# FFN weights loaded first and quantised as they land; V copied from PSUM by ScalarE, its bias folded into the output projection's

## What is computed

```
def fp4_linear(x, w):
    xq = fp4_quant_dequant(x)
    wq = fp4_quant_dequant(w)
    return einsum('bsk,nk->bsn', xq, wq)
...
v = (x @ Wv + bv).reshape(Bb, Ss, H, HD)
...
attn = softmax(scores, axis=-1)
out = einsum('bhts,bshd->bthd', attn, v).reshape(Bb, Ss, Dd)
return out @ Wo + bo
```

## Time and profile before

| | |
|---|---|
| median of 3 runs | 4952.22 us (4935.51, 4952.22, 4952.87) |
| the profiled execution | 4937.85 us, of which the span from first to last instruction is 4936.0 us |
| mean granted TensorE clock | 0.907 |
| TensorE busy | 3986.5 us (81%) |
| VectorE busy | 4018.3 us (81%) |
| ScalarE busy | 2381.1 us (48%) |
| GpSimd busy | 1575.5 us (32%) |
| the chain that ended last | PE 38%, DVE 38%, ACT 11%, issue 4%, DMA 4%, SPq 3% |

### The profile page before, as it was taken

How to read it: one execution, slowest core, us unless ns; L and a number is a source line. 1 busy time by engine, 2 the same in 40 slices (tenths; PEclk the granted TensorE clock), 3 DMA queues, 4 the chain that set the end, 5 groups by cost and what they waited for, 6 DMA issues and landing times.

```text
span 4936.0 us, 53882 instructions
## 1 busy us (share of the span) xinstructions
PE 3986.5 (81%) x18173; PEld 2036.9 (41%) x18173; DVE 4018.3 (81%) x5964; ACT 2381.1 (48%) x4341; POOL 1575.5 (32%) x1036
## 2 busy tenths in 40 slices
PE   3456768898988888888988888888989888877767
PEld 1222324353535444443535444443535344434343
DVE  5487879898898989899898989898988989785512
ACT  1334344546545465545555464645465454543332
POOL 0043333333433333333433333333334333333000
PEclk9667879999999999999999999999999999898877
DMA  1387666767767776767777677677677677774100
GB/s 56 82 181 186 147 169 157 181 162 169 179 149 184 160 184 163 175 163 171 177 159 177 157 186 171 165 169 179 170 163 176 152 185 161 182 175 92 41 22 29
DMA packets 241433, 753.39 MB, mean 153 GB/s; under 512 B 37650, under 2 KB 132659, under 8 KB 171524
## 3 DMA queue, kind: packets, MB, share of 16 engines
q1 hardware_dynamic: 241156, 749.95, 63.5%
HBM read 647.30 MB, written 101.71 MB: 152 GB/s over the span
## 4 chain that ended last, share of the span: by engine, by line
PE 38%; DVE 38%; ACT 11%; issue 4%; DMA 4%; SPq 3%; POOL 1%; DVEq 0%; ACTq 0%; POOLq 0%
DVE state L1559 9%; PE m L1087 7%; DVE mt L1647 6%; PE m L1059 6%; DVE u L1554 5%; DVE front L1496 2%; PE m L1099 2%; DVE front L1381 2%; SPq L551 2%; PE pd L1284 2%; DMA dt_scratch<-front 2%; PE y L1162 2%; DVE front L1383 2%; DVE front L1469 1%; DVE front L1472 1%
## 5 line engine op out<-in xcount | busy, mean ns | idle before, releaser
L708 POOL TENSOR_TENSOR state<-state,bc 128x1024 f32<-128x1024 f32 x512 | 1216.2, 2376 | 1886.2 <-DVE u L1554 1886.2
L1559 DVE TENSOR_TENSOR_SCAN state<-decay,u 128x1024 f32<-128x1024 f32 x512 | 1169.2, 2284 | 24.0 <-ACT decay L878 11.1
L878 ACT ACTIVATE decay<-decay,a_neg 128x511 f32<-128x511 f32 x1024 | 670.1, 711 | 169.5 <-DMA decay<-dt_scratch 168.8
L1059 PE MATMUL m<-w_gu,hats_m 128*128 128x480 f32 (+1 forms) x1536 | 686.4, 579 | 28.9 <-DVE front L1472 23.1
L1554 DVE TENSOR_TENSOR u<-state,bc 128x1024 f32<-128x1024 f32 x512 | 645.5, 1261 | 44.4 <-DMA state<-dtx_scratch 36.5
L1087 PE MATMUL m<-w_dn,front 128*128 128x256 f32 (+1 forms) x1536 | 424.7, 423 | 17.9 <-ACT front L814 16.4
L692 POOL TENSOR_TENSOR front<-front,hsc_m 128x704 f32<-128x704 f32 x128 | 192.0, 1500 | 728.0 <-DVE front L1383 728.0
L1059 PEld LDWEIGHTS m<-w_gu,hats_m 128*128 128x128 f32 x1536 | 281.7, 195 | 300.4 <-issue 208.3
L1151 PE MATMUL y<-state,sel 128*32 128x512 f32 x2048 | 290.9, 651 | 122.5 <-POOL state L708 121.7
L795 ACT ACTIVATE front<-m 128x240 f32<-128x240 f32 (+1 forms) x384 | 137.2, 362 | 500.4 <-PE m L1059 478.0
L1087 PEld LDWEIGHTS m<-w_dn,front 128*128 128x128 f32 (+1 forms) x1536 | 301.5, 208 | 141.0 <-issue 65.7
(11 more groups left out here) (260 smaller groups left out, 7112.8 us busy)
## 6 DMA issues: line engine op xcount, KB each, us to landing
decay<-dt_scratch SPq DMA_DIRECT2D x256, 1024.0 KB, 7.2
state<-dtx_scratch SPq DMA_DIRECT2D x256, 1024.0 KB, 11.3
qk_scratch<-shared SPq DMA_DIRECT2D x64, 384.0 KB, 3.5
shared<-qk_scratch SPq DMA_DIRECT2D x384, 64.0 KB
kh<-qk_scratch SPq DMA_DIRECT2D x384, 64.0 KB
xs_scratch<-front SPq DMA_DIRECT2D x16, 1024.0 KB, 6.0
dt_scratch<-front SPq DMA_DIRECT2D x256, 64.0 KB, 2.0
dtx_scratch<-hats_m SPq DMA_DIRECT2D x256, 64.0 KB, 1.7
```

Of the source, the lines that this page charges most:

```text
L708: eng.tensor_tensor(st, st, bc[:, 1:2, :].to_broadcast([P, WIDE, L]), ALU.mult).then_inc(scan_pool.sem, scan_pool.step(f"c{r}{h}"))
L878: ins = eng.activation(d, d, ACT.Exp, scale=a_neg[:, g:g + 1])
L1059: mm = eng.matmul(f.bank(f"gu{t}{p}")[:, 0:2 * width], f.norm.hat_t[:, k, t * P:(t + 1) * P], w_gu[:, k, 2 * lo:2 * (lo + width)], start=( ...
L1559: eng.tensor_tensor_scan(st, decay[:, n % ND, h * WIDE * L:(h + 1) * WIDE * L], u[:, :], 0.0, ALU.mult, ALU.add).then_inc(scan_dve.sem, sc ...
```

## The change

1. The loads of the three FFN weights are issued ahead of the first sequence, and each weight has a semaphore of its own (`raw_loaded`). VectorE waits for that alone before it quantises a weight; its wait for `loaded` and the small copy `raw_by_state` come after the three. TensorE and ScalarE still wait for all of `loaded` at their start.
2. `bv` is loaded as a column per feature, and `bo` as one row. In the setup TensorE computes `bv @ Wo + bo` (three matmuls, 1x256), ScalarE copies it into `bo`, and only then comes the rest of ScalarE's setup.
3. V is copied from PSUM by ScalarE instead of being added to `bv` by VectorE. The plan tables are unchanged, so that the four copies have no entry in `ACT_PLAN`.

```diff
-            load(xx[:, 0, :, :], a["x"][0].rearrange("(t p) d -> p t d", p=P))
             for name, src in (("gate", a["w_gate"]), ("up", a["w_up"])):
                 dst = raw[name].rearrange("p (k d) -> p k d", k=IK)
-                load(dst[:, 0:IK - 1, :], src[0:(IK - 1) * P, :].rearrange("(k p) d -> p k d", p=P))
-                load(dst[0:IL, IK - 1, :], src[(IK - 1) * P:I, :])
-            load(raw["down"].rearrange("p (k d) -> p k d", k=KD), a["w_down"].rearrange("(k p) d -> p k d", p=P))
+                eng.dma_start(dst[:, 0:IK - 1, :], src[0:(IK - 1) * P, :].rearrange("(k p) d -> p k d", p=P)).then_inc(raw_loaded[name], 16)
+                eng.dma_start(dst[0:IL, IK - 1, :], src[(IK - 1) * P:I, :]).then_inc(raw_loaded[name], 16)
+            eng.dma_start(raw["down"].rearrange("p (k d) -> p k d", k=KD), a["w_down"].rearrange("(k p) d -> p k d", p=P)
+                          ).then_inc(raw_loaded["down"], 16)
+            load(xx[:, 0, :, :], a["x"][0].rearrange("(t p) d -> p t d", p=P))
...
-            load(bv[:, :], a["bv"].rearrange("(o d) -> o d", o=1).to_broadcast([P, D]))
-            load(bo[:, :], a["bo"].rearrange("(o d) -> o d", o=1).to_broadcast([P, D]))
+            load(bv[:, :], a["bv"].rearrange("(k p) -> p k", p=P))
+            load(bo[:, :], a["bo"].rearrange("(o d) -> o d", o=1))
...
+            n += 1
+            eng.wait_ge(set_pe, n + 1)
+            eng.activation(bo[0:1, :], RB[n % 4][0:1, 0:D], ACT.Copy).then_inc(set_act, 1)
             eng.wait_ge(set_act, 2 + n)
             eng.mul(a_neg[:, :], a_neg[:, :], -1.0)
...
+                for t in range(T):
+                    yield 19 + t
+                    if t == 0 and r:
+                        eng.wait_ge(att_pe.sem, att_pe.after(r - 1, f"p{J - 1}{T - 1}{G - 1}"))
+                    eng.wait_ge(att_pe.sem, att_pe.after(r, f"v{t}"))
+                    eng.activation(va[:, t, :, 0:HD], (PD, PG)[t % 2][:, 0:D].rearrange("p (h r) -> p h r", r=HD), ACT.Copy
+                                   ).then_inc(att_act.sem, att_act.step(f"v{t}"))
...
+            eng.wait_ge(set_dve, SET_QUANTISED["down"] + 1)
             eng.transpose(RB[n % 4][:, P:P + C * Q * Q], raw_by_state, ident[0:C * Q * Q, 0:C * Q * Q]).then_inc(set_pe, 1)
+            n += 1
+            free(n)
+            for k in range(KD):
+                eng.matmul(RB[n % 4][0:1, 0:D], bv[:, k:k + 1], w_o[:, k, :], start=(k == 0), stop=False)
+            eng.matmul(RB[n % 4][0:1, 0:D], ident[0:1, 0:1], bo[0:1, :], start=False, stop=True).then_inc(set_pe, 1)
...
                     if t >= 2:
-                        eng.wait_ge(att_dve.sem, att_dve.after(r, f"v{t - 2}"))
+                        eng.wait_ge(att_act.sem, att_act.after(r, f"v{t - 2}"))
...
                         if k == 0 and g == 0:
                             mine["pd"] = True
-                            eng.wait_ge(att_dve.sem, att_dve.after(r, f"v{T - 1}"))
+                            eng.wait_ge(att_act.sem, att_act.after(r, f"v{T - 1}"))
...
-            eng.wait_ge(loaded, 16 * n_loads[0])
             eng.wait_ge(set_pool, 1)
             wait()
-            eng.tensor_copy(raw_by_state.rearrange("g (s e) -> g s e", e=E8), raw_a.rearrange("g (e s) -> g s e", e=E8)).then_inc(*mark(0))
             small = [f.qs[:, n, :] for n in range(4)]
             half = T * D // QB
             for which in ("gate", "up", "down"):
                 width = IK * D if which != "down" else KD * I
+                eng.wait_ge(raw_loaded[which], 32 if which != "down" else 16)
...
+            eng.wait_ge(loaded, 16 * n_loads[0])
+            eng.tensor_copy(raw_by_state.rearrange("g (s e) -> g s e", e=E8), raw_a.rearrange("g (e s) -> g s e", e=E8)).then_inc(*mark(0))
...
-                for t in range(T):
-                    yield 19 + t
-                    if t == 0 and r:
-
-                        eng.wait_ge(att_pe.sem, att_pe.after(r - 1, f"p{J - 1}{T - 1}{G - 1}"))
-                    eng.wait_ge(att_pe.sem, att_pe.after(r, f"v{t}"))
-                    eng.tensor_tensor(va[:, t, :, 0:HD], (PD, PG)[t % 2][:, 0:D].rearrange("p (h r) -> p h r", r=HD),
-                                      bv[:, :].rearrange("p (h r) -> p h r", r=HD), ALU.add).then_inc(att_dve.sem, att_dve.step(f"v{t}"))
-
```

More of the change, by code:

```diff
@@ L119, in build @@
         w_lb = sb("w_lb", [E * R + 1, D])
-        bv = sb("bv", [P, D])
-        bo = sb("bo", [P, D])
+        bv = sb("bv", [P, KD])
+        bo = sb("bo", [1, D])
         rb = sb("rb", [P, E])
@@ L246, in build @@
         loaded = sem("loaded")
+        raw_loaded = {which: sem(f"raw_loaded_{which}") for which in ("gate", "up", "down")}
         set_dve, set_act, set_pe, set_pool = sem("set_dve"), sem("set_act"), sem("set_pe"), sem("set_pool")
@@ L290, in build @@
                        + ["a0", "a1"] + [f"o{t}" for t in range(T)])
-        att_act = Steps(sem("att_act"), ["x0", "x1"] + [n for n_ in range(4) for n in (f"one{n_}", f"two{n_}", f"three{n_}")]
+        att_act = Steps(sem("att_act"), ["x0", "x1"] + [n for n_ in range(4) for n in (f"one{n_}", f"two{n_}", f"three{n_}")] + [f"v{t}" for t in range(T)]
                         + [n for k in range(NG) for n in (scores_of(k) if kind(k)[0] == "e" else []) + act_after(k)] + ["a0", "a1", "res0", "res1"])
-        att_dve = Steps(sem("att_dve"), [f"v{t}" for t in range(T)]
-                        + [n for k in range(NG) for n in (scores_of(k) + ([f"m{w}{kind(k)[1]}" for w in "abcd"] if kind(k)[2] == T - 1 else [])
+        att_dve = Steps(sem("att_dve"), [n for k in range(NG) for n in (scores_of(k) + ([f"m{w}{kind(k)[1]}" for w in "abcd"] if kind(k)[2] == T - 1 else [])
                                                          if kind(k)[0] == "s" else []) + [m for w in after_group(k) if w[:2] == "ot" for m in (f"rec{w[2]}", f"att{w[2]}")]])
@@ L328, in spread @@
             return ap.rearrange("p (n o) -> p n o", o=1).to_broadcast([P, n, QB])
-        SET_QUANTISED = {"gate": 30, "up": 50, "down": 70}
+        SET_QUANTISED = {"gate": 29, "up": 49, "down": 69}
         SET_DVE = 76
@@ L759, in _ @@
             eng.mul(vec[:, 0:20], vec[:, 0:20], 0.5).then_inc(set_act, 1)
-            assert n == 16
+            assert n == 17
             def hats(n, q, x):
@@ L1423, in _ @@
             assert at[0] == SET_DVE
-            eng.wait_ge(set_act, 19)
+            eng.wait_ge(set_act, 20)
             def norm(n, q, x):
```

## The result

The changed kernel takes 5016.98 us (median of 4 runs, 5000.17 to 5028.01) against 4952.55 (median of 4, 4935.51 to 4953.99). The ratio is 1.0136, 95% interval 1.0119 to 1.0154: slower by 67 us (1.36% of 4952.55; the medians themselves are 64 apart). The prediction was 5022, in 4960 to 5050, slower with a chance of 0.81.

The account below looks back on a forecast made before the run. No single engine bounds it: TensorE and VectorE, each busy 81%, share the chain. Fourteen periods at +6.7 us, less 15.9 for setup, give +78: 5016 or 5030 from two base times, middle 5022, its own range 5001 to 5049, stated range 4960 to 5050.

Parts of the forecast that it names:

- The setup: Program start: quantisation begins at 7.0 instead of 24.19 us, gaining 17.2; bias product costs 1.3; in all -15.9 us.
- The fold: End of setup: three added fp32 matmuls and one ScalarE row copy for the bias cost 1.3 us.
- v2, the transposes, v3: TensorE at V: v2 starts at 2730.9 instead of 2729.23, transposes at 2734.6 instead of 2733.76, v3 at 2735.6.
- The decays and L776: ScalarE at V: five decays and the transposes' copy wait behind v3's copy, making the first gate/up matmul 5.2 us late.
- The clock at the place: Gate/up matmuls after V: a 4.7 us idle gap halves TensorE's clock for 5.2 us, costing 2.6 us.
- The period: One V to the next, 276.06 us before: grows by 4.1 + 2.6 = 6.7 us, range 5.8 to 7.9.
- if TensorE keeps its clock: Each period, from the late gate/up matmul less TensorE's 1.04 us idle: grows by 4.1 us without a clock fall.
- The sum: Whole kernel: 14 periods at 6.7 us, 93.8, less 15.9 for the setup, +78 us; last two sequences count nothing.
- Rival 1: Gate/up after V: clock holds or falls too briefly to matter; +41.5 us, 4979 to 4994; chance 0.15.
- Rival 2: After V: only VectorE's 1.9 us scan delay carries through the period; +11 us, 4949 to 4963; chance 0.08.
- Rival 3: Around V: faster, delay lies in slack and VectorE keeps its saving; -33 us, 4905 to 4919; chance 0.10.
- Rival 4: Later in each period: late periods bring more low clock; over 8 us a period, above 5050 us; chance 0.05.

Follow-up runs that it names:

- e3: The changed kernel with V copied from PSUM by VectorE again, early start and folded bias kept: 4940.31 us, ratio 0.9988 to the kernel before.
- e1: The kernel before with only the FFN weight loads issued first and quantised as they land, bias and V copies as before: 4931.28 us, ratio 0.9973.
- e9: The changed kernel with 20 filler matmuls behind the last V product and 10 more ahead of the third: 5004.89 us, ratio 1.0127 to the kernel before.
- e4: The changed kernel with 20 filler matmuls on TensorE behind the last V product: 5017.77 us, ratio 1.0144 to the kernel before.
- e6b: The changed kernel with v2's copy behind ScalarE's five decays and v3's behind L776, ahead of the tanhs: 4941.19 us, ratio 0.9984 to the kernel before.
- e7b: e6b with the last q/k copy and the first two V copies also ahead of ScalarE's size evacuation: 4948.28 us, ratio 1.0016 to the kernel before.
- e8: e7b with 20 fillers in place of 12 ahead of the back FFN's transposes: 4949.04 us, ratio 1.0004 to the kernel before.
- e10: e6b with 10 more fillers ahead of V's third product: 4954.33 us, ratio 1.0011 to the kernel before.
- e5b: The changed kernel with the copies of V's third and fourth tile behind ScalarE's five decays: 4955.53 us, ratio 1.0018 to the kernel before.

## Why the prediction was right, point by point

**The setup, -15.9 predicted.** Measured 15.33 to the first layer norm (69.84 to 54.51). Two errors nearly cancel. The start was put at 7.0 and came at 6.03, 1 us better. The DMA view of the first 30 us has the gate's load (KB, us from issue to landing):

```profile
state<-in_w_gate_dram SPq DMA_DIRECT2D x1, 640.0 KB, 4.7
```

The start at 6.03 is within the 5.8 to 7.0 that I had worked out from the rule of the Trainium skill (DMA: Bandwidth & Descriptors, section "Two DMAs through the same engine are not ordered"), from which I took that the gate weights don't share with later ones. That section says only that descriptors in one queue of one engine start in order; that the gate's load then lands as if it were alone was my inference, and 4.7 us for 640 KB, beside the 4.6 for 512 KB, fit it. My middle between landing alone and sharing was the wrong choice. The fold was put at 1.3. In e3 it cost 1.31. In the changed kernel it cost 2.2 (54.51 - 52.19 of e1, less 0.10 that e1 started earlier, at 5.93): the four records of its first two matmuls took 1.86 us, in e3 1.02. It isn't the clock, which is 1.00 over both; why it is so wasn't tested. Another 0.6 us were not in the sum at all: e1 has no fold, starts 18.26 us earlier and reaches the layer norm 17.65 earlier.

**v2, the transposes, v3.** Laid on each other at the start of the quantisation (2725.44 before, 2761.81 after, 36.37 apart), v2 starts 1.60 us later (predicted 1.67), the transposes 0.63 later (0.84), v3 0.03 later (0.4).

**The decays and L776.** The gate/up product is 4.58 us late (2777.15 - 36.37 = 2740.78, against 2736.20). I had said 5.2. I had laid copy, decays and copy end to end; on ScalarE the next instruction starts before the row of the last one ends (2772.70 + 0.38 is 2773.08, the decays begin at 2772.98; they end at 2776.13, L776 begins at 2776.03). That is 0.2 of the 0.6; the rest is v3, which was 0.37 earlier than I had said. In the other kind of place the product is 17.02 - 10.76 = 6.26 late. The sum has no such place: it saw v2 start 1.67 late, and not that the clock could fall behind the wait ahead of it.

**The clock at the place, 2.6 us predicted.** The gap is 4.49 (4.7 said). The product takes 2.72 us longer, 6.10 for 3.38. The idle 1.04 ahead of the sum over states is used up as said: of 4.58 + 2.72 = 7.30, 5.72 are left at the row maxima (2789.20 - 36.37 = 2752.83, against 2747.11); the sum said 6.7 there. At this place the mechanism and both its terms are right, the total 1.0 too high. Where the clock has fallen ahead of the transposes, the product takes 5.07 to 5.16 us instead of 6.06 to 6.23, and the row maxima come only some 0.3 later than at the first kind.

**The period.** By the ratio, 67 us lost and 15.3 won in the setup make 82, over 14 periods 5.9 each, where 6.7 was said. The profiled pair has 7.8, in part since the changed kernel's profile is of the slowest of its runs and that of before of one of the fastest. Of these 7.8, 6.3 arise between the start of the quantisation and the row maximum at 2798.14 (36.61 us in the mean over the twelve periods, 30.35 before), and 1.5 in the rest of the period (245.55, 244.04 before). How much is the wait and how much the clock can be tried at equal time at half clock. Before's four periods with 30.7 us of it last 276.0 to 276.8; e9's ten with about that last 279.5 to 280.2, and so does the changed kernel's only one (279.8). Difference: **3.5 us**, against the 4.1 of "if TensorE keeps its clock". The rest, 2.4 by the ratio and 4.3 in the profiled pair, would go with the clock, against 2.6. This split isn't firm: at about 37.5 us of half clock before has one period, of 277.4, and the changed kernel six, of 280.3 to 283.2, so that the difference there is 2.9 to 5.8. Nor is it the price at the place alone: e4 took away the 2.7 us there and saved nothing in the whole, so the step "TensorE is the late engine, each us at half clock costs half a us" holds locally and not over the period.

**The sum.** The total owes something to luck. I had said +78 us on a kernel before of 4944; it was +64 on one of 4952.55 (+67 by the ratio). The one is 11 to 14 too high, the other 8 to 9 too low, and 5022 lies nearer to 5016.98 than either term to its own. The clock's share of a period was priced at one place, which e4 shows to be the wrong way to price it.

**What half clock costs, from before's own periods.** Seven with 20.4 to 23.9 us at half clock last 272.0 to 273.5, mean 272.9; the four with 30.7 last 276.3 in the mean, and one with 37.5 lasts 277.4. Some 9 us more at the lower level go with 3.4 us more time. The mean of the twelve is 274.4; the 276.06 that the prediction took for the period is of the longer kind.

**The rivals.** Rival 1 (the clock holds) falls with the windows above; its 4979 to 4994 lies under all four runs. Rival 2 falls too: the delay isn't VectorE's 1.9 alone. Rival 3, faster because VectorE keeps what it saves, falls in a stronger sense than the prediction had: even with the copies well placed (e6b, e7b) the additions saved on VectorE buy no time of a run that can be measured; e7b's 0.45 us at the place are lost again in the rest of the period. Rival 4, more low clock in later stretches, has the right mechanism in part (39.2 us for 25.8 per period), and not the size.

**A mistake in the words.** The FFN around V is the back FFN of the next sequence, which the fillers' name `"back x"` says too, not a front FFN, as the text ahead of the prediction has it. No number hangs on it.

**Still open.** Why seven of before's twelve periods have some 20 to 24 us at half clock and the others 30.7 or more, in the same instructions; why the places at V are of two kinds; and why the versions with V well placed on ScalarE (e6b, e7b, e8, e10) have few of the short kind.

## What to carry to other kernels

When an operation goes to an engine with a fixed order, price what stands behind it there, not its duration: these copies are 0.04 us shorter than the additions, and one of them made five decays and an evacuation wait 4 us. One number of the order, which moved two of the copies (e5b), took the period back from 282.2 to 276.4 us, where it had been 274.4; the relief of the other engine, busy for 81%, shows in no run's time. A change that bundles a gain at the start with a move in the loop is worth taking apart: the reordered loads alone have the lowest times here, 0.3 to 0.4% under the kernel before, in two series of runs, though e3 and e6b aren't told apart from the first of them.

## What was not expected of the hardware

- Filling an idle stretch of TensorE kept the granted clock up at that place and let it fall some 25 us later, for 13.6 us (e4, summed over windows of 1 us). The Trainium skill (TensorE: Matmul & The Clock Gate, section "HAM oscillation — how this bites in real kernels") has idle gaps put the clock back; the 4.49 us gap agrees. In six of the first thirteen places of the changed kernel the clock fell behind a shorter one too, the 2.25 us ahead of v2, and in seven it did not. In e4 it fell in 2796 to 2800, where TensorE was busy for 2.11 of 4 us, and stood at 0.50 over 2800 to 2808, where it was busy for 3.66 and 3.54.
- One program has periods of two lengths, 3.4 us apart, with 20 to 24 or 31 us at half clock. Runs of e6b spread over 1% (4907.25 to 4956.04), at a mean clock of 0.905 and 0.893.
